# Causal attention in a post-norm decoder layer: scores computed once, by query rows in 32-row array tiles, and the softmax weights turned by DMA

## The chip, the cores and the metric

The kernel runs on one core of a Trainium2 chip. The metric is the device time of one execution in microseconds; lower is better. The five engines that matter are TensorE (PE), VectorE (DVE), ScalarE (ACT), GpSimd (POOL) and SyncE (SP), each with its own in-order instruction stream; they meet in semaphores. Moves between memories, and transposes done on the way, are DMAs.

## The reference

A decoder layer on `x` (4 x 512 x 512) in fp32: causal self-attention with 16 heads of 32, cross-attention with a 512 x 256 context, and a gated feed-forward with ternary weights, each followed by a residual and a layer norm.

```
Q = (X @ Wq.T + bq).reshape(B, S, H, d_head) * scale      # K likewise, V without scale
scores = jnp.einsum('bqhd,bkhd->bhqk', Q, K)
causal = jnp.tril(jnp.ones((S, S), bool))
scores = jnp.where(causal[None, None], scores, -jnp.inf)
attn = jax.nn.softmax(scores, axis=-1)
out = jnp.einsum('bhqk,bkhd->bqhd', attn, V).reshape(B, S, D)
x = _layernorm(x + out @ Wo.T + bo)
# cross-attention: energy = (ctx Wq)(ctx Wk)^T, softmax, x_m = x @ attention; x = _layernorm(x + x_m)
# ffn: xq = quantised rms_norm(x); p = silu(xq @ sign(W_g).T) * (xq @ sign(W_u).T); p @ sign(W_d).T
x = _layernorm(x + ffn)
```

## The kernel before

**Halves and steps.** The work is cut into eight steps `s`: batch `s // 2`, and in it the first or second 256 positions (`h = s % 2`). fp32 values are carried as a high and a low fp16 part, and a product is three matmuls (high x high, low x high, high x low); the helper at line 700 records all of those of the projections. Heads come in four groups `g` of four heads `j`; one group's queries and keys fill 128 partitions, 32 for each head. `gp` is a pair of groups.

**Causal attention before.** Queries and keys (`project`, `qk`) land in `qk`. SyncE then copies them (`stack`, line 635, tasks `sk`) into `st`, so that for each head 96 partitions hold high, low and high parts: one matmul with a depth of 96 gives the three products at once. The scores are computed twice. First by query rows (`score_max`, lines 753 and 757, tasks `mx`): only to get each query's maximum, which VectorE takes under the causal mask (`block_max`, line 1122). The maxima of two groups are turned by a small transpose (`maxima`, line 764, tasks `nm`), split in two, and copied as rows 96 and 97 of `st` by DMA (`shift_rows`, line 643, tasks `sh`), beside a constant on the key side (`shift_constants`). Then by key columns (`scores`, line 774, tasks `st`), with a depth of 128 that takes the maximum away in the product. ScalarE exponentiates. Where a piece has the diagonal, the result goes to `p32`, GpSimd masks it (`mask`, line 1274), ScalarE writes the high part into `ph` and GpSimd the low one. Where it has none, ScalarE exponentiates twice (`open_exponentials`, lines 960 and 961) and VectorE writes the low part (line 1060). As keys are on the partitions already, `ph` is the stationary operand of the product with `v` (`weigh`, line 795, tasks `pv`).

**The rest.** `op` is the output projection, `cp`, `en`, `xm` the cross-attention, `gg`, `uu` (line 851) and `dn` (line 866) the feed-forward; `to`, `tx`, `ta`, `tq` are DMA transposes of `ohl`, `rhl`, `ehl`, `xq`. All of SyncE's DMAs go through one queue.

**Order.** Each engine runs a list written out in the file (`PE_ORDER`, `ACT_ORDER`, ...), in which attention of one batch lies among the feed-forward of the batch before. Words are task and arguments; a number behind `@` is the PSUM bank, of which there are eight. A bank is reopened when the task that had it has been read (`freed_by`).

## Time and profile before

| | |
|---|---|
| median of 3 runs | 623.63 us (620.34 to 623.85) |
| the profiled execution | 617.3 us of span; 6.3 us less than the median run, which is the time around it |
| PE busy | 583.5 us, 95% |
| DVE busy | 487.6 us, 79% |
| ACT busy | 413.0 us, 67% |
| POOL busy | 395.0 us, 64% |
| DMA queue of SP | 36.4% of 16 engines' span |

The span is the profiled part of one execution. An engine's busy time is the union of its instructions. Matmuls are pipelined, so their mean duration is a latency, and what one costs in a stream is read from the length of a run of them. The granted clock of 1.00 is 2.4 GHz.

### The profile page before, as it was taken

What the parts mean: (1) busy time and instruction counts of PE and PEld (TensorE: products, weight loads), DVE (VectorE), ACT (ScalarE), POOL (GpSimd) and SP (SyncE); (2) the same over time, 40 slices, a digit from 0 to 9 for tenths busy, and PEclk for the clock granted to TensorE, in tenths of its full rate; (3) what the DMA queues carried; (4) which work ended last, traced back from release to release, by engine and by line L of the source; (5) the groups of instructions that cost most, each with busy time, mean ns of one, the idle gap of its engine ahead of it and who ended that gap; (6) DMA issues with size and microseconds to landing.
All of it is one profiled execution on the core that took longest, in us unless ns stands there. A gap on an engine that the chain in (4) does not pass through costs nothing.

```text
span 617.3 us, 13871 instructions
## 1 busy us (share of the span) xinstructions
PE 583.5 (95%) x5100; PEld 389.1 (63%) x5100; DVE 487.6 (79%) x1296; ACT 413.0 (67%) x773; POOL 395.0 (64%) x518
## 2 busy tenths in 40 slices
PE   5699789999999999989999999999999999999996
PEld 4466556547766667747666676786666667685572
DVE  3767677798998966688799886778798898787775
ACT  5849979946676776945675977655656778854151
POOL 9343966655676867665875894626876667767443
PEclk9999869999999999999999999999999999999999
DMA  8867952594024321163312520044122431032000
GB/s 302 323 206 230 253 174 53 129 256 86 10 47 105 91 70 37 49 158 91 78 39 46 146 69 19 3 103 120 36 51 53 105 87 36 10 90 56 19 35 34
DMA packets 90851, 60.29 MB, mean 98 GB/s; under 512 B 65056, under 2 KB 81952, under 8 KB 89248
## 3 DMA queue, kind: packets, MB, share of 16 engines
q1 hardware_dynamic: 90240, 58.89, 36.4%
q8 instruction: 40, 0.66, 0.5%
q10 hardware_dynamic: 544, 0.52, 0.3%
q14 instruction: 27, 0.22, 0.1%
HBM read 27.79 MB, written 4.19 MB: 52 GB/s over the span
## 4 chain that ended last, share of the span: by engine, by line
PE 66%; SPq 11%; DMA 6%; DVE 6%; ACT 6%; issue 3%; POOL 2%; ACTq 0%; POOLq 0%; DVEq 0%
PE ps_b L700 24%; PE ps_b L851 16%; PE ps_b L866 14%; SPq L635 9%; PE ps_b L795 4%; PE ps_b L774 4%; PE ps_b L757 2%; DMA st<-qk 2%; PE ps_b L753 1%; DMA oT<-ohl 1%; DMA bx<-in_b_x_dram 1%; DVE ps_b L1122 1%; ACT ps_b L961 1%; ACT p L947 1%; ACT ph L884 1%
## 5 line engine op out<-in xcount | busy, mean ns | idle before, releaser
L1122 DVE CUSTOM_DVE_ANT_0 ps_b<-ps_b,future 128x256 f32<-128x256 f32 (+3 forms) x256 | 118.7, 517 | 16.9 <-PE ps_b L757 10.4
L1317 POOL TENSOR_TENSOR ph<-p,ph 128x512 f16<-128x512 f32 x96 | 110.0, 1161 | 27.2 <-ACT ph L884 26.5
L851 PE MATMUL ps_b<-xqT,sg 128*128 128x256 f16 x1024 | 124.9, 272 | 0.1
L866 PE MATMUL ps_b<-sd,hp 128*128 128x512 fp8e4 x512 | 119.1, 379 | 0.0
L1313 POOL TENSOR_TENSOR hp<-gt,hp 128x512 f16<-128x512 f32 x64 | 74.0, 1161 | 56.6 <-ACT hp L884 56.2
L851 PEld LDWEIGHTS ps_b<-xqT,sg 128*128 128x128 fp8e4 x1024 | 98.0, 98 | 19.0 <-ACT p L947 0.6
L700 PE MATMUL ps_b<-xhl,wh 128*128 128x256 f16 x480 | 84.8, 275 | 1.4 <-DVE wl L1073 1.3
L866 PEld LDWEIGHTS ps_b<-sd,hp 128*128 128x128 f16 x512 | 48.6, 98 | 50.0 <-POOL hp L1313 1.5
L1274 POOL TENSOR_SCALAR_AFFINE_SELECT p<-p 128x256 f32<-128x256 f32 (+1 forms) x96 | 46.5, 494 | 46.2 <-ACT p L947 45.7
L700 PE MATMUL ps_b<-xhl,wl 128*128 128x256 f16 x240 | 66.0, 275 | 0.0
L947 ACT ACTIVATE p<-ps_b 128x512 f32<-128x512 f32 x96 | 54.1, 594 | 16.8 <-PE ps_b L774 16.5
L884 ACT ACTIVATE ph<-p 128x512 f16<-128x512 f32 x96 | 58.0, 634 | 9.3 <-POOL p L1274 9.0
L884 ACT ACTIVATE hp<-gt 128x512 f16<-128x512 f32 x64 | 39.9, 628 | 30.8 <-DVE gt L1239 28.1
L1060 DVE TENSOR_TENSOR ph<-ps_b,ph 128x512 f16<-128x512 f32 x64 | 43.2, 685 | 20.9 <-ACT ps_b L961 20.9
L774 PE MATMUL ps_b<-st 128*128 128x256 f16 (+1 forms) x384 | 53.9, 260 | 1.7 <-DVE tops L1122 1.2
L1032 ACT ACTIVATE gt<-gt 128x512 f32<-128x512 f32 x64 | 40.1, 626 | 19.5 <-DVE gt L1226 18.9
L700 PEld LDWEIGHTS ps_b<-xhl,wh 128*128 128x128 f16 x480 | 47.3, 99 | 9.1 <-DVE wl L1073 1.9
L1231 DVE SCALAR_TENSOR_TENSOR gt<-gt,ps_b 128x512 f32<-128x512 f32 x64 | 43.6, 682 | 11.6 <-ACT gt L1032 11.0
L1226 DVE TENSOR_TENSOR gt<-ps_b,invb 128x512 f32<-128x512 f32 x64 | 43.6, 686 | 9.6 <-POOL hp L1313 5.9
L795 PEld LDWEIGHTS ps_b<-v,ph 128*128 128x128 f16 x1376 | 46.4, 97 | 6.4 <-DVE tops L1122 1.2
L795 PE MATMUL ps_b<-v,ph 128*128 128x65 f16 (+2 forms) x1376 | 48.5, 184 | 0.5 <-DVE ph L1060 0.3
L1239 DVE SCALAR_TENSOR_TENSOR gt<-gt,ps_b 128x512 f32<-128x512 f32 x64 | 43.1, 682 | 5.4 <-PE ps_b L851 4.5
(122 smaller groups left out, 1139.6 us busy)
## 6 DMA issues: line engine op xcount, KB each, us to landing
st<-qk SPq DMA_DIRECT2D x192, 64.0 KB, 2.0
hp<-in_sgT_dram SPq DMA_DIRECT2D x6, 1024.0 KB, 6.8
gt<-in_sgT_dram SPq DMA_DIRECT2D x6, 1024.0 KB, 6.0
rows<-in_x_dram SPq DMA_DIRECT2D x8, 512.0 KB, 3.8
out_dram<-rows SPq DMA_DIRECT2D x16, 256.0 KB, 2.1
xin<-in_xT_dram SPq DMA_DIRECT2D x14, 256.0 KB, 4.5
e<-in_ctxT_dram SPq DMA_DIRECT2D x4, 512.0 KB, 4.2
hp<-in_wT_dram SPq DMA_DIRECT2D x4, 256.0 KB, 4.4
```

The costliest lines, as they stand in the source:

```text
L635: sp.dma_start(st[DH * r:DH * (r + 1), q:k + 1:k - q, j, :, :], qk[DH * j:DH * (j + 1), gp, first:first + step + 1:step, :, :])\
L700: ins = pe.matmul(ps, lhs(hl, c), rhs(hr, c), start=n == 0, stop=n == len(todo) - 1)
L774: ins = pe.matmul(ps[:, col:col + HALF - first], st[:, Q_SLOTS + 2 * gp + kt // 2, j, g % 2, kt % 2 * P:(kt % 2 + 1) * P], st[:, (2 * s + ...
L795: ins = pe.matmul(ps[:, col:col + width], ph[:, n % PH_SLOTS, half, at:at + P], v[:, kt, HG * g + j, first:first + width], start=kt == hal ...
L851: ins = pe.matmul(ps[:, a * HALF:(a + 1) * HALF], sg[:, ("gg", "uu").index(name), c, ht * P:(ht + 1) * P], xqT[:, c, :], start=c == 0, sto ...
L866: ins = pe.matmul(ps[:, :], hp[:, (UNITS * s + n) % HP_SLOTS, h, a, t * P:(t + 1) * P], sd[:, ht, :], start=ht == h == 0, stop=ht == HT - ...
L884: act.activation(out_, in_, ACT.Copy, scale=scale).then_inc(signal, 1)
L947: act.activation(p32[:, m % P32_SLOTS, :], ps[:, :], ACT.Exp, scale=EXP_SCALE).then_inc(p_exp.sem, 1)
L1122: ins = dve.tensor_tensor_reduce(scores, scores, future[:, S - width:S], 1.0, -3e38, ALU.add, ALU.max, tops[:, g // 2, j:j + 1, g % 2, qt ...
L1274: pool.affine_select(out=blocks, in_=blocks, pattern=[[0, len(cols)], [1, P]], compare_op=ALU.is_ge, fill=0.0, base=0, channel_multiplier= ...
L1313: pool.tensor_tensor(slot[:, 1, :, :], tg[:, n % 2, :, :], slot[:, 0, :, :], ALU.subtract)\
L1317: pool.tensor_tensor(out_, in_, hi, ALU.subtract).then_inc(signal, 1)
```

## The change

Scores are computed once, by query rows. There is no stacking: the three products are three matmuls with a depth of 32, each on one head's 32 partitions, and the four heads of a group follow each other, in four row tiles of the array and into four banks. Wq and bq are taken with a minus sign, so that VectorE's reduction (a minimum now) gives the exponential's bias as it is; its masked and scaled scores go back to PSUM, and ScalarE exponentiates those with the bias. Two heads make a pair (`pair`): one `p32` slot, one high part (ScalarE writes that of pair 0, VectorE that of pair 1) and one low part (GpSimd). As the queries are on the partitions now, SyncE turns both halves by one DMA transpose for each pair (`turn_weights`, tasks `tp`) into `pt`, which is what `weigh` reads. Gone are `stack`, `maxima`, `shift_rows`, `mask`, `open_exponentials`, and the second set of scores. All order lists are written anew. The buffers change with it: `p32` has 3 slots, `ph` 3, `pt` 5.

```diff
-Q_SLOTS, K_SLOTS = 3, 4
-P32_SLOTS, PH_SLOTS, HP_SLOTS = 4, 10, 6
+Q_SLOTS, K_SLOTS = 2, 3
+P32_SLOTS, PH_SLOTS, PT_SLOTS, HP_SLOTS = 3, 3, 5, 6
+FIRST_WIDTH = P + HALF
+def tiles_of(s, i):
+    return ((0, 0, P), (1, P, HALF)) if s % 2 == 0 else ((3 - i, 0, (4 - i) * P),)
+def width_of(s, i):
+    return FIRST_WIDTH if s % 2 == 0 else (4 - i) * P
...
             if name == "mx":
-                return bm_red, 0, before(MX_PIECES, s, *parts) + 1
+                return p_exp, 0, pieces_to(s, *parts) + 1
...
         def ph_free(eng, n):
 
             if n >= PH_SLOTS:
-                s0, g0, k0 = place_of(n - PH_SLOTS)
-                wait(eng, pv_done, s0, HG * g0 + LAST_HEAD[s0 % 2][k0] + 1)
+                wait(eng, turned[(n - PH_SLOTS) % PT_SLOTS], (n - PH_SLOTS) // PT_SLOTS, 16)
...
-            def stack(s, gp, j):
...
-            def shift_rows(s, gp):
...
+            def turn_weights(s, g, i, pair):
+                n, blocks = pairs_to(s, g, i, pair), 4 * width_of(s, i) // P
+                wait(sp, p_lo, 0, n + 1)
+                if n >= PT_SLOTS:
+                    s0, g0, _, pair0 = pair_at(n - PT_SLOTS)
+                    wait(sp, pv_done, s0, HG * g0 + 2 * pair0 + 2)
+                sp.dma_start_transpose(pt[:, n % PT_SLOTS, 0:blocks, :], ph[:, n % PH_SLOTS, 0:blocks * P])\
+                  .then_inc(turned[n % PT_SLOTS].sem, 16)
...
+            def scores(s, g, i):
+                h = s % 2
+                wait(pe, qk_lo, s, 2 * g + 2)
+                banks = [open_bank(("mx", s, g, HG * i + j)) for j in range(HG)]
+                for qt, col, width in tiles_of(s, i):
+                    for hq, hk in ((0, 0), (0, 1), (1, 0)):
+                        for kh in range((width + HALF - 1) // HALF):
+                            keys = min(width - kh * HALF, HALF)
+                            first = hq == hk == kh == 0 and col == 0
+                            last = hq == 1 and kh == (width - 1) // HALF and col + width == width_of(s, i)
+                            for j in range(HG):
+                                mine = slice(DH * j, DH * (j + 1))
+                                ins = pe.matmul(banks[j][:, col + kh * HALF:col + kh * HALF + keys],
+                                                qs[mine, s % Q_SLOTS, g, hq, qt % 2 * P:(qt % 2 + 1) * P],
+                                                ks[mine, (s - h + kh) % K_SLOTS, g, hk, 0:keys],
+                                                start=first, stop=last, skip_group_check=True)
+                                if last:
+                                    done(ins, ("mx", s, g, HG * i + j))
...
+                    n = pairs_to(s, g, (3 - qt) * h, j // 2)
+                    wait(pe, turned[n % PT_SLOTS], n // PT_SLOTS, 16)
                     for kt in range(qt + 1):
-                        k, at = p_block(h, j, kt, qt)
-                        n = before(ST_PIECES, s, g, k)
-                        wait(pe, *low_of(n))
                         for half, first, width in products_of:
-                            ins = pe.matmul(ps[:, col:col + width], ph[:, n % PH_SLOTS, half, at:at + P],
+                            ins = pe.matmul(ps[:, col:col + width], pt[:, n % PT_SLOTS, p_block(s, j, qt, kt, half), :],
...
             def exponentials(s, g, k):
+                i, j = divmod(k, HG)
+                n, width = pairs_to(s, g, i, j // 2), width_of(s, i)
+                act.wait_ge(*filled("mx", s, g, k))
+                ps = bank_of("mx", s, g, k)
+                wait(act, bm_red, 0, pieces_to(s, g, k) + 1)
+                wait(act, p_lo, 0, n - P32_SLOTS + 1)
+                for qt, col, keys in tiles_of(s, i):
+                    to = j % 2 * width + col
+                    ins = act.activation(p32[:, n % P32_SLOTS, to:to + keys], ps[:, col:col + keys], ACT.Exp, scale=-1.0,
+                                         bias=tops[:, s % 2, g, j, qt % 2:qt % 2 + 1])
+                ins.then_inc(p_exp.sem, 1)
...
-            def open_exponentials(s, g, k):
...
             def block_max(s, g, k):
+                i, j = divmod(k, HG)
...
+                if s >= 2:
+                    wait(dve, p_exp, 0, pieces_to(s - 2, g, HG * (1 + s % 2)))
+                for qt, col, width in tiles_of(s, i):
                     scores = ps[:, col:col + width]
-                    ins = dve.tensor_tensor_reduce(scores, scores, future[:, S - width:S], 1.0, -3e38, ALU.add, ALU.max,
-                                                   tops[:, g // 2, j:j + 1, g % 2, qt % 2])
+                    ins = dve.tensor_tensor_reduce(scores, scores, future[:, S - width:S], EXP_SCALE, 3e38, ALU.add, ALU.min,
+                                                   tops[:, s % 2, g, j, qt % 2:qt % 2 + 1])
                 ins.then_inc(bm_red.sem, 1)
...
+            def p_high(s, g, i, pair):
+                n, width = pairs_to(s, g, i, pair), 2 * width_of(s, i)
+                wait(dve, p_exp, 0, pieces_to(s, g, HG * i + 2 * pair + 2))
+                ph_free(dve, n)
+                dve.tensor_copy(ph[:, n % PH_SLOTS, 0:width], p32[:, n % P32_SLOTS, 0:width]).then_inc(p_hi[1].sem, 1)
...
-            def mask(s, g, k):
...
+            def p_low(s, g, i, pair):
+                n, width = pairs_to(s, g, i, pair), 2 * width_of(s, i)
+                wait(pool, p_hi[pair], 0, n // 2 + 1)
+                hi, lo = (ph[:, n % PH_SLOTS, half * width:(half + 1) * width] for half in range(2))
+                low(lo, p32[:, n % P32_SLOTS, 0:width], hi, p_lo.sem)
```

Two pieces of the new PE list show the two kinds of surroundings (`mx` with its four banks):

```
mx0.1.1.0@6,0,1,5 pv0.0.3.0@7 pv0.0.3.1@7 pv0.0.3.2@7 pv0.0.3.3@7 qk1.0.0@2 mx0.1.1.1@7,6,4,3 qk1.0.1@0 qk1.0.2@5
...
dn0.1.0.0@1 va1.1.1@2 mx1.1.1.0@4,3,5,6 dn0.1.0.1@1 uu0.1.4@7 uu0.1.7@3 op1.0.0@5 mx1.1.1.1@2,6,7,0 pv1.1.0.0@4
```

## Rows read from the trace of the kernel before

**Rows 1.** The page: busy time, share of the span, instructions of each engine.

```profile
PE 583.5 (95%) x5100; PEld 389.1 (63%) x5100; DVE 487.6 (79%) x1296; ACT 413.0 (67%) x773; POOL 395.0 (64%) x518
```

**Rows 2.** Windows: busy time of each engine in a stretch, TensorE clock, DMA share.

```profile
core 0: us, PE busy (x) PEld busy (x) DVE busy (x) ACT busy (x) POOL busy (x), PEclk, DMA share, GB/s
0.00:120.00 120.00, 97.84 (x899) 65.70 (x900) 81.65 (x246) 95.85 (x177) 74.56 (x83) 0.94 0.70 210
120.00:560.00 440.00, 434.37 (x3892) 292.80 (x3888) 365.69 (x976) 297.86 (x567) 294.26 (x396) 1.00 0.32 75
560.00:617.00 57.00, 51.31 (x318) 30.61 (x316) 40.26 (x75) 19.30 (x31) 26.16 (x41) 0.98 0.12 33
```

**Rows 3.** Windows again, two shorter stretches.

```profile
60.00:90.00 30.00, 24.66 (x237) 16.39 (x237) 22.20 (x73) 25.29 (x47) 23.50 (x29) 0.77 0.87 241
...
300.00:400.00 100.00, 99.26 (x942) 67.05 (x940) 86.08 (x206) 74.93 (x144) 72.08 (x95) 1.00 0.23 56
```

**Rows 4.** Timeline of PE: start us, length us, then the run of like matmuls.

```profile
341.53 0.39 PE L774 MATMUL ps_b<-st 128*128 128x128 f16 x4
...
547.57 1.79 PE L795 MATMUL ps_b<-v,ph 128*128 128x65 f16 x60
...
583.26 13.26 PE L851 MATMUL ps_b<-xqT,sg 128*128 128x256 f16 x120
...
600.69 10.62 PE L866 MATMUL ps_b<-sd,hp 128*128 128x512 fp8e4 x48
```

**Rows 5.** Groups of PE: busy us, mean ns of one.

```profile
L851 PE MATMUL ps_b<-xqT,sg 128*128 128x256 f16 x1024 | 124.9, 272 | 0.1
L851 PEld LDWEIGHTS ps_b<-xqT,sg 128*128 128x128 fp8e4 x1024 | 98.0, 98 | 19.0 <-ACT p L947 0.6
...
L764 PE MATMUL ps_b<-ident,tops 128*16 128x128 f32 x16 | 4.4, 273 | 0.2
```

**Rows 6.** Windows of the instructions on tile st alone, from 120 us on.

```profile
120.00:617.00 497.00, 75.08 (x520) 42.70 (x520) 0.00 (x0) 1.00 0.29 71
```

**Rows 7.** Groups of DVE, ACT and POOL by form: busy us, mean ns of one.

```profile
L1060 DVE TENSOR_TENSOR ph<-ps_b,ph 128x512 f16<-128x512 f32 x64 | 43.2, 685 | 20.9 <-ACT ps_b L961 20.9
L1209 DVE TENSOR_SCALAR scaled<-rows,amax 128x512 f32<-128x512 f32 x16 | 8.6, 538 | 0.6
...
L884 ACT ACTIVATE ph<-p 128x512 f16<-128x512 f32 x96 | 58.0, 634 | 9.3 <-POOL p L1274 9.0 <-PE ps_b L795 0.2
L947 ACT ACTIVATE p<-ps_b 128x512 f32<-128x512 f32 x96 | 54.1, 594 | 16.8 <-PE ps_b L774 16.5
L961 ACT ACTIVATE ps_b<-ps_b 128x512 f32<-128x512 f32 x64 | 38.7, 605 | 0.0
L884 ACT ACTIVATE invb<-ps_b 128x256 f32<-128x256 f32 x8 | 3.1, 382 | 8.0 <-PE ps_b L840 6.7 <-DVE gt L1226 1.3
...
L1317 POOL TENSOR_TENSOR ph<-p,ph 128x512 f16<-128x512 f32 x96 | 110.0, 1161 | 27.2 <-ACT ph L884 26.5
L1274 POOL TENSOR_SCALAR_AFFINE_SELECT p<-p 128x256 f32<-128x256 f32 (+1 forms) x96 | 46.5, 494 | 46.2 <-ACT p L947 45.7
```

**Rows 8.** DMA issues: count, KB each where shown, median us from issue to landing.

```profile
st<-qk SPq DMA_DIRECT2D x192, 64.0 KB, 2.0
...
oT<-ohl SPq DMA_TRANSPOSE x16, 3.3
...
xqT<-xq SPq DMA_TRANSPOSE x16, 2.4
```

**Rows 9.** SyncE's issuing instructions: min, median, max ns, first and last start.

```profile
L635 SPq DMA_DIRECT2D st<-qk x192: 585/597/1647, 26.8 to 483.1; - x192
...
L646 SPq DMA_TRANSPOSE oT<-ohl x16: 1232/1302/1977, 105.1 to 554.3; - x16
```

**Rows 10.** The chain that ended last, in order of time, 27 to 49 us: two pieces.

```profile
42.51 0.61 SPq L635
43.16 6.06 DMA st<-qk
```

More of the change, by code:

```diff
@@ new lines, in width_of, with pieces_to, pairs_to, pair_at @@
+def width_of(s, i):
+    return FIRST_WIDTH if s % 2 == 0 else (4 - i) * P
+def pieces_to(s, g, k):
+    per = (HG, 2 * HG)
+    return NG * (s // 2 * sum(per) + s % 2 * per[0]) + g * per[s % 2] + k
+def pairs_to(s, g, i, pair):
+    per = (2, 4)
+    return NG * (s // 2 * sum(per) + s % 2 * per[0]) + g * per[s % 2] + 2 * i + pair
+def pair_at(n):
+    b, n = divmod(n, NG * 6)
+    h = int(n >= NG * 2)
+    g, n = divmod(n - h * NG * 2, 2 + 2 * h)
+    return 2 * b + h, g, *divmod(n, 2)
+def p_block(s, j, qt, kt, half):
+    blocks = width_of(s, 3 - qt) // P
+    first = 0 if s % 2 or qt == 0 else 1
+    return (2 * half + j % 2) * blocks + first + kt
@@ L347, in read_order @@
             args = (2 * args[0] + args[1], *args[2:])
-        steps.append((word[:2], args, int(bank) if bank else None))
+        steps.append((word[:2], args, tuple(map(int, banks.split(","))) if banks else ()))
     return steps
@@ L354, in place_uses @@
     place, users, fills = {}, [[] for _ in range(8)], [0] * 8
-    for name, args, bank in order:
-        if bank is None:
-            continue
-        task = (name, *args[:2]) if name in ("pv", "dn") else (name, *args)
-        if task not in place:
-            fills[bank] += name not in ("pv", "dn")
-            place[task] = (bank, len(users[bank]), fills[bank])
-            users[bank].append(task)
+    for name, args, banks in order:
+        for j, bank in enumerate(banks):
+            task = (name, *args[:2]) if name in ("pv", "dn") else (name, *args)
+            if name == "mx":
+                task = (name, *args[:2], HG * args[2] + j)
+            if task not in place:
+                fills[bank] += name not in ("pv", "dn")
+                place[task] = (bank, len(users[bank]), fills[bank])
+                users[bank].append(task)
     return place, users
@@ L545, in at @@
                 return 1
-        def low_of(n):
-            where = place_of(n)
-            return p_lo if has_diagonal(where[0], where[2]) else q_lo, 0, among(*where) + 1
         def blocks_of(ps, first, blocks, width):
@@ L963, in low_products @@
+            def p_high(s, g, i, pair):
+                n, width = pairs_to(s, g, i, pair), 2 * width_of(s, i)
+                wait(act, p_exp, 0, pieces_to(s, g, HG * i + 2 * pair + 2))
+                ph_free(act, n)
+                split(ph[:, n % PH_SLOTS, 0:width], p32[:, n % P32_SLOTS, 0:width], p_hi[0].sem)
             def low_products(s, g):
@@ L1268, in _ @@
         def _(pool):
-            def mask(s, g, k):
-                m = among(s, g, k)
-                wait(pool, p_exp, 0, m + 1)
-                cols = [col for _, _, col in ST_PIECES[s % 2][k]]
-                blocks = p32[:, m % P32_SLOTS, :].rearrange("p (n q) -> p n q", n=len(cols))[:, :, 0:P]
-                pool.affine_select(out=blocks, in_=blocks, pattern=[[0, len(cols)], [1, P]], compare_op=ALU.is_ge,
-                                   fill=0.0, base=0, channel_multiplier=-1).then_inc(p_mask.sem, 1)
             def spread(s, t):
```

612 lines of the change are left out of this document (225 added, 387 removed).

## The prediction

> **What bounds the kernel now.** First the busy times [rows 1]: PE at 95% is far ahead of DVE at 79%. A mean over the span can hide stages, so next the windows [rows 2]. From 120 to 560 us PE is busy 434.4 of 440 us at the full clock: there it is the bound, with nothing to fill. In the first 120 us it idles 22.2 us, and in the last 57 us, feed-forward and last norm of the last half, 5.7 us. Two shorter windows [rows 3] say what stands behind PE: at 300 to 400 us DVE is busy 86%, ACT 75%, POOL 72%; and from 60 to 90 us, where the first attention runs with little else, PE has 82% and the clock fell to a mean of 0.77, between the levels 1.2 and 2.4 GHz, after PE had idled. So TensorE time taken away between 120 and 560 us is worth its full length as long as DVE and the chains between the engines let PE stay dense; what is taken away before 120 us is worth little.
>
> **What a matmul costs in a stream.** Durations are latencies (272 ns for 256 columns [rows 5]), so I read lengths of runs [rows 4]. 120 matmuls of 256 columns take 13.26 us; less one latency, (13.26 - 0.27) / 119 = 0.109 us each. 48 of 512 columns take 10.62 us, 0.22 each, twice that (0.218). 128 columns: 0.055, and four take 0.39 = 3 x 0.055 + 0.22, the last one's latency. 60 of 65 columns or fewer take 1.79 us: 0.027 each beside a tail of 0.2. As each of these has a weight load of its own, 0.027 us is also the least that a pair of load and matmul costs here.
>
> **Removed from PE.** For each of 64 heads and batches, row scores had one matmul of 512, two of 256 and two of 128 columns, column scores four of 256 and two of 128. 64 x 0.218 + 384 x 0.109 + 256 x 0.055 = 14.0 + 41.9 + 14.1 = 70.0 us. 16 turns of the maxima (`nm`), 0.11 each in a stream, at most their latency of 0.273 [rows 5]: 1.8. Together 71.8 us.
>
> **Added to PE.** A batch and group has 24 matmuls of 32 rows in the first half (12 of 128 columns, 12 of 256) and 48 in the second (12 of 128, 36 of 256): 1152 in all, in 288 rounds of four heads, 192 rounds of 256 and 96 of 128 columns. No matmul of the trace runs in a 32-row tile, so I bound this from both sides. If the four of a round run side by side, a round of 256 costs what one such matmul costs, 0.109 us, and it can't issue faster than 4 x 0.027 = 0.108: 0.109. A round of 128 then costs 0.108 by issue, 0.055 by columns. 192 x 0.109 + 96 x 0.108 = 31.3 us; low end 192 x 0.109 + 96 x 0.055 = 26.2. If the four run one after another, 768 x 0.109 + 384 x 0.055 = 104.8. I take 31.3: heads differ in rows of the array and in banks, so nothing that they write or hold is shared.
>
> **Going in and out of tiles.** 48 steps of scores lie among full-array matmuls, so the array changes its shape 96 times. The trace has no such change. Below, it costs nothing. Above, the full matmul before must end, 0.272 - 0.109 = 0.163 us beyond its stream price, and the next weight load (0.098 [rows 5]) is no longer hidden: 0.261. I take the first part, 96 x 0.163 = 15.6 us, since the loads fill rows that are free by then; ends 0 and 25.1. For this a rule exists: the Trainium skill, TensorEngine Tiling (Array Packing), Key Properties, says that changing the tiling mode drains TensorE. It speaks against the change as interleaved here; without it the sum would be better by those 15.6 us. A second one speaks against full overlap: the Trainium skill, TensorE: Matmul & The Clock Gate, Measured speedup vs the span model, has 3.07x for four row tiles; by that, my estimate is 104.8 / 3.07 = 34.1 us in place of 31.3. No row here shows either.
>
> So PE does 31.3 + 15.6 = 46.9 in place of 71.8: **-24.9 us**, ends -45.6 (26.2, no drain) and -15.4 (31.3 and 25.1). Of the 704 removed score matmuls 520 lie behind 120 us [rows 6], 74%: **-18.4 us** in the dense part; the other 6.5 fall where PE has idle time to spare, and I count them as nothing.
>
> **The other engines** [rows 7]. DVE: off go 64 low parts at 0.685 (43.8) and 16 maxima at about 0.27 (4.3). The 256 reductions keep their widths. On come 48 copies of 768 (32) and 1024 columns (16); the nearest row, 512 columns in 0.538, scales to 0.81 and 1.08: 43 us (if a plain copy were twice as fast, 22). DVE stays at 483 us, 82% of a shorter span. ACT: off go 96 x 0.594 + 96 x 0.634 + 64 x 1.21 + 4 = 199; on come 64 exponentials of each of 128, 256, 384 and 512 columns (from 0.594 and 0.382 by width, 0.28 + 0.38 + 0.49 + 0.59), 111, and 48 high parts at 0.85 to 1.06, 44: -44 us, off the path. POOL: off go 96 masks (96 x 0.494 = 47) and 96 x 1.161 = 111; on come 64 x 1.74 + 32 x 2.32 = 186 at most, in proportion to width: +27, 422 us, 70%. None of them overtakes PE. ACT's two added waits (`bm_red`, then `p_lo`) stand ahead of FFN work in its list, as does DVE's wait for ScalarE's exponentials of two halves before; that last one has long been met.
>
> **The queue of SyncE.** Off go 192 stack copies at 0.60 of issue (115 us) and 32 of maxima (19) [rows 9]; on come 96 transposes at 1.30 (125): even. Moved data: a transpose of 4 blocks lands after 2.4 us, one of 8 after 3.3 [rows 8], some 0.2 us for a block, so 12 blocks land after some 4.2 us and 16 after 5.1. 1280 new blocks are up to 256 us of the DMA engines, against a share of 0.32 in use in the dense part: up to 0.75, less the stacks. That hides. In the first 120 us it doesn't quite: the share is 0.70, 84 us [rows 2], for the sign matrices are loaded then; the first batch brings 320 blocks, 64 us, for stacks that took perhaps 12; that is 136 us of demand in 120. Part can slip behind 120 us; I put **+4 us**, ends 0 and +16. Against it, the first scores no longer wait for the last of the stacks in the chain: issues from 27 to 43 us and then 6.06 us of landing [rows 10]. The wait for the projections remains, so I take **-4 us**, ends 0 and -6.
>
> **Waits added.** A weight now passes reduction, exponential, high part, low part, issue and a landing of some 4 to 5 us before `pv`. SyncE's `turn_weights` waits for GpSimd's low part, and behind it in one queue stand `tq` and `to`, for which `gg` and `op` wait, and loads of `x`. A `ph` slot is held for about 1.06 + 2.32 + 1.3 + 5.1 = 9.8 us, three slots give a pair every 3.3 us; a batch has 24 pairs, 78 us in some 145, enough but not idle. Four banks at once are held through four reductions. In the dense part PE idles 1.3% now; I let that rise by a percent, **+4 us**.
>
> **The sum.** 617.3 - 18.4 + 4 - 4 + 4 = 602.9 us of span, and with 6.4 us around it (623.6 less 617.3): **609 us**, 2.3% under the median. 1% is about what a measurement of this kernel can tell from no change.
>
> **The rivals.** (1) *The shape changes cost nothing* and rounds of 128 run at column pace. Then the whole -45.6 stands, 34 of it in the dense part, and the time is about 617.3 - 34 + 4 + 6.4 = 594. For it: tiles of other rows can load while the last full matmul drains. Against: DVE, 86% at 300 to 400 us, would be the next bound.
>
> (2) *PE starves in the dense part*: the long way from scores to `pv`, with three slots and one in-order queue for all transposes, opens gaps wherever another engine runs late. It decides from the point where the idle time between 120 and 560 us grows from 5.6 by more than the 18.4 us that are saved, to above 24, or 5.5%. PE's idle share between 0 and 120 us is 18.5%, and between 60 and 90 us, where attention alone feeds it, also 18%; if the attention stretches of the later batches had 7% of idle over the 440 us, that is 31 us, 25 more than now: 617.3 - 18.4 + 25 + 6.4 = 630, slower than before. For it: five engines in a row for each pair, and the clock that fell after idle time [rows 3]. Against: some 55% of PE's work is feed-forward and projection, which the lists lay between the steps.
>
> (3) *The row tiles don't overlap*: 104.8 + 15.6 in place of 71.8 is +48.6 us, all of it on PE: 617.3 + 48.6 + 6.4 = 672. Nothing in this trace speaks against it but that the banks and rows are separate.
>
> **How the numbers follow.** Forecast (600 to 622): 0.45. Rival 1 (580 to 600): 0.15. Rival 2 (613 to 645): 0.27. Rival 3: 0.13. The range of 8 in 10 leaves rival 3 out, and tips of the others: 583 to 643. Faster by over 1% (under 617.4): 0.38 + 0.15 + 0.02 = 0.55. Within 1%: 0.07 + 0.07 = 0.14. Slower (over 629.9): 0.18 + 0.13 = 0.31. The forecast's and rival 1's own range is 583 to 620.
>
> **What would show it.** The form 32*128 in the groups of PE: in its timeline, four such matmuls of 256 columns per 0.11 us, or per 0.44 if rival 3 holds; a gap of some 0.16 us at each end of a step. Windows 120 to 560 us: PE busy near 97% is the forecast; under 94% is rival 2, and then the waits of PE name `pt` or the banks of the scores. The DMA share there near 0.6. DVE near 483, POOL near 420, ACT near 370 us. It would be wrong most simply if a short matmul in a tile can't issue at 0.027 us: each 0.01 us more for one is 11.5 us.

## The result: 0.8% slower

| | before | after |
|---|---|---|
| median of 5 runs each | 621.45 us (620.34 to 623.85) | 626.21 us (624.83 to 627.64) |
| profiled execution, span | 617.3 us | 624.2 us |

The ratio is 1.0079, with an interval of 1.0051 to 1.0107: slower, by less than the 1% called "within" in the prediction, which had forecast 609 us, against a median before of 623.6 (three runs then, five now). The first line of the page answers to [rows 1], the windows to [rows 2] and [rows 3] (share of DMA engines in the last column but one, after the granted clock):

```profile
PE 552.5 (89%) x5532; PEld 352.1 (56%) x5532; DVE 494.7 (79%) x1264; ACT 396.3 (63%) x741; POOL 408.1 (65%) x421
...
q1 hardware_dynamic: 240768, 88.11, 70.0%
```

```profile
core 0: us, PE busy (x) PEld busy (x) DVE busy (x) ACT busy (x) POOL busy (x), PEclk, DMA share, GB/s
0.00:120.00 120.00, 88.13 (x895) 56.45 (x896) 75.77 (x216) 89.75 (x159) 56.66 (x53) 0.86 1.01 256
120.00:560.00 440.00, 406.36 (x4287) 261.69 (x4286) 374.07 (x968) 284.25 (x547) 320.10 (x324) 0.99 0.71 128
560.00:624.00 64.00, 58.03 (x354) 33.92 (x352) 44.90 (x82) 22.29 (x35) 31.35 (x45) 1.00 0.13 38
...
60.00:120.00 60.00, 40.65 (x447) 25.63 (x448) 32.66 (x88) 38.84 (x57) 31.15 (x22) 0.74 1.10 235
120.00:140.00 20.00, 11.49 (x183) 8.59 (x182) 15.41 (x54) 14.94 (x25) 15.08 (x18) 0.74 0.88 155
240.00:320.00 80.00, 70.41 (x852) 45.19 (x850) 70.59 (x210) 51.37 (x109) 61.72 (x67) 1.00 0.86 152
```

PE's busy time shrank as meant, 583.5 to 552.5 us, 31.0 less, and the span still grew by 6.9: the idle time of PE grew by 37.9. Of that, 28.0 lie between 120 and 560 us (440 - 406.4 = 33.6 in place of 5.6) and 9.7 in the first 120 us (31.9 in place of 22.2), where the clock's mean is 0.86 and the DMA engines have no time left (share 1.01). The worst stretch behind that is the next one, 120 to 140 us: 8.5 of 20 us idle, at a clock of 0.74. Later the idle time is spread; from 240 to 320 us it is 9.6 us, and no other engine is full there (DVE 88%, POOL 77%).

The new matmuls, first in PE's timeline (start, length, count of a run), then by form, as in [rows 4] and [rows 5]:

```profile
301.68 0.50 PE L704 MATMUL ps_b<-v,pt 128*128 128x65 f16 x12 [0.50 <-DVE ks L1004]
302.11 0.83 PE L682 MATMUL ps_b<-ks,qs 32*128 32x256 f16 x24
302.87 0.54 PE L704 MATMUL ps_b<-v,pt 128*128 128x65 f16 x14
...
447.02 0.27 PE L626 MATMUL ps_b<-xhl,wl 128*128 128x256 f16 x1
447.13 0.27 PE L626 MATMUL ps_b<-xhl,wh 128*128 128x256 f16 x1
447.33 0.67 PE L682 MATMUL ps_b<-ks,qs 32*128 32x128 f16 x24
447.94 0.28 PE L626 MATMUL ps_b<-xhl,wh 128*128 128x256 f16 x1
```

```profile
L682 PE MATMUL ps_b<-ks,qs 32*128 32x256 f16 x768 | 34.3, 289 | 17.6 <-DVE o L1043 8.1 <-ACT p L853 8.0 <-DVE gt L1126 0.8
L682 PE MATMUL ps_b<-ks,qs 32*128 32x128 f16 x384 | 15.4, 224 | 2.2 <-DVE rows L1073 1.0 <-DVE rows L1142 0.8 <-ACT p L853 0.3
```

24 tile matmuls of 256 columns, six rounds of four heads, stand 0.76 us before the next full-array matmul starts; at 0.109 a round they need 0.65. So the four run side by side, and going out of the tiles leaves 0.11 us. Going in costs about as much and lies before the first tile matmul: at 447 us the full-array matmuls of 256 columns start 0.11 us apart, and the first tile matmul starts 0.20 us after the last of them, 0.09 later than in a stream. So a change of shape costs some 0.1 us here, not 0.163. The second step (its row names the first form only) has three rounds of 128 columns and three of 256 in 0.61 us; less 3 x 0.109 and the 0.11 for going out, a round of 128 takes some 0.06 us, the pace of its columns (0.055) and not the 0.108 taken for issue.

What waits, and for what: SyncE's queue, then DVE, then PE (us in total, times, longest).

```profile
SPq L568 <- POOL ph L1203: 146.7, 64, 12.8
...
DVE gt L1121 <- POOL hp L1199: 19.0, 27, 1.7
...
PE ps_b L682 <- ACT p L853: 8.3, 4, 5.6
PE ps_b L682 <- DVE o L1043: 8.1, 2, 6.1
PE ps_b L704 <- DMA pt<-ph: 6.8, 7, 3.2
```

The turns themselves, as in [rows 9] (issue in ns: min, median, max), and the groups of GpSimd, VectorE and ScalarE that stand before them, as in [rows 7]:

```profile
L568 SPq DMA_TRANSPOSE pt<-ph x96: 1274/1776/8447, 38.2 to 542.2; - x96
...
DMA to landing us min/median/max: 3.6/4.3/10.4
```

```profile
L1203 POOL TENSOR_TENSOR ph<-p,ph 128x768 f16<-128x768 f32 x64 | 105.6, 1653 | 40.6 <-ACT ph L793 22.6 <-DVE ph L1030 17.9
...
L1203 POOL TENSOR_TENSOR ph<-p,ph 128x1024 f16<-128x1024 f32 x32 | 68.7, 2148 | 28.9 <-ACT ph L793 21.4 <-DVE ph L1030 7.5
...
L1030 DVE CAST ph<-p 128x768 f16<-128x768 f32 x32 | 28.0, 876 | 8.0 <-ACT p L853 5.3 <-DMA pt<-ph 2.6
L1030 DVE CAST ph<-p 128x1024 f16<-128x1024 f32 x16 | 20.2, 1264 | 5.5 <-ACT p L853 5.4
...
L853 ACT ACTIVATE p<-ps_b,tops 128x512 f32<-128x512 f32 x64 | 41.8, 686 | 22.8 <-DVE tops L1022 9.8 <-issue 5.0 <-POOL ph L1203 4.6
```

SyncE's one queue stands 146.7 us before the turns (L568), waiting for GpSimd's low parts, and behind each such wait are `tq`, `to`, `tx` and the loads of `x`. A queue that stands has lost nothing by that alone: in the kernel before it waited for GpSimd as well, 54.2 us for the low parts of `rhl` alone. The three waits of PE are 23 us of the 71.7 that it idles; its idle time is spread over many names, so the waits alone don't say which link to shorten. Experiments have to.

### The profile page after: what moved, and what is told of

Same layout as the page of the kernel before. It is cut to its first block and busy times, and to the rows that moved or that the text cites. A ratio compares the mean times of both kernels' runs of the same rounds, so it can differ in the third digit from the quotient of the medians.

```text
span 624.2 us, 14611 instructions
## 1 busy us (share of the span) xinstructions
PE 552.5 (89%) x5532; PEld 352.1 (56%) x5532; DVE 494.7 (79%) x1264; ACT 396.3 (63%) x741; POOL 408.1 (65%) x421
## 5 line engine op out<-in xcount | busy, mean ns | idle before, releaser
L1203 POOL TENSOR_TENSOR ph<-p,ph 128x768 f16<-128x768 f32 (+1 forms) x96 | 174.1, 1818 | 69.5 <-ACT ph L793 43.9
L853 ACT ACTIVATE p<-ps_b,tops 128x128 f32<-128x128 f32 (+3 forms) x256 | 119.9, 535 | 51.4 <-DVE tops L1022 27.5
L1022 DVE CUSTOM_DVE_ANT_0 ps_b<-ps_b,future 128x128 f32<-128x128 f32 (+3 forms) x256 | 117.9, 518 | 17.5 <-PE ps_b L682 17.3
L760 PE MATMUL ps_b<-xqT,sg 128*128 128x256 f16 x1024 | 119.7, 273 | 4.5 <-DVE o L1043 1.0
L1199 POOL TENSOR_TENSOR hp<-gt,hp 128x512 f16<-128x512 f32 x64 | 76.1, 1196 | 47.6 <-ACT hp L793 47.6
L704 PE MATMUL ps_b<-v,pt 128*128 128x65 f16 (+2 forms) x1376 | 48.4, 186 | 16.1 <-DMA pt<-ph 6.8
L704 PEld LDWEIGHTS ps_b<-v,pt 128*128 128x128 f16 x1376 | 44.9, 98 | 30.1 <-ACT p L853 9.6
L793 ACT ACTIVATE hp<-gt 128x512 f16<-128x512 f32 x64 | 39.9, 628 | 33.6 <-DVE gt L1134 32.4
L1030 DVE CAST ph<-p 128x768 f16<-128x768 f32 (+1 forms) x48 | 48.2, 1005 | 13.6 <-ACT p L853 10.7
L682 PE MATMUL ps_b<-ks,qs 32*128 32x256 f16 (+1 forms) x1152 | 38.2, 267 | 19.8 <-ACT p L853 8.3
L626 PE MATMUL ps_b<-aT,x1T 128*128 128x512 f16 x192 | 45.5, 392 | 1.3 <-ACT p L853 0.7
L793 ACT ACTIVATE ph<-p 128x768 f16<-128x768 f32 (+1 forms) x48 | 44.2, 921 | 0.2
```

What stands on the lines that cost most here:

```text
L626: ins = pe.matmul(ps, lhs(hl, c), rhs(hr, c), start=n == 0, stop=n == len(todo) - 1)
L704: ins = pe.matmul(ps[:, col:col + width], pt[:, n % PT_SLOTS, p_block(s, j, qt, kt, half), :], v[:, kt, HG * g + j, first:first + width], ...
L760: ins = pe.matmul(ps[:, a * HALF:(a + 1) * HALF], sg[:, ("gg", "uu").index(name), c, ht * P:(ht + 1) * P], xqT[:, c, :], start=c == 0, sto ...
L793: act.activation(out_, in_, ACT.Copy, scale=scale).then_inc(signal, 1)
L853: ins = act.activation(p32[:, n % P32_SLOTS, to:to + keys], ps[:, col:col + keys], ACT.Exp, scale=-1.0, bias=tops[:, s % 2, g, j, qt % 2:q ...
L1022: ins = dve.tensor_tensor_reduce(scores, scores, future[:, S - width:S], EXP_SCALE, 3e38, ALU.add, ALU.min, tops[:, s % 2, g, j, qt % 2:qt ...
```

## Experiments

Ratios are to the kernel before, in runs on the same chip; times are medians. The changed kernel stands at 626.2 (1.0079, interval 1.0051 to 1.0107), the one before at 621.5. The experiments ran on several chips, on which the kernel before had medians of 620.3 to 621.6 us; where two kernels below differ by less than about 3 us and their intervals overlap, the difference isn't shown.

### Which part of the changed kernel costs: one at a time

**quarter_turns** turns 4 blocks in place of 12 or 16, so that `pv` reads the wrong blocks.

```diff
-sp.dma_start_transpose(pt[:, n % PT_SLOTS, 0:blocks, :], ph[:, n % PH_SLOTS, 0:blocks * P])
+sp.dma_start_transpose(pt[:, n % PT_SLOTS, 0:4, :], ph[:, n % PH_SLOTS, 0:4 * P])
```

> Leaves out: each weight transpose moves only its first 4 blocks of 12 or 16, and the weighted sums read those 4 again and again. All waits, issues and matmuls stay. Theory A (the volume of the transposes is what starves PE: DMA share above 1.0 up to 120 us, 0.71 behind it): the DMA share falls to about 0.4, the waits of the weighted sums for pt go, and the time falls from 626 to 600 us or less. Theory B (the chain of reduction, exponential, high and low part on DVE, ACT and POOL starves it): within 5 us of 626, only the first 140 us gain a little. Theory C (PE itself): no change.

623.35 us, 1.0025 (1.0002 to 1.0048). The DMA share from 120 to 560 us fell to 0.37 and SyncE's issue by a third, which answers to the row of L568 above:

```profile
L568 SPq DMA_TRANSPOSE pt<-ph x96: 1188/1190/2905, 38.0 to 538.8; - x96
```

Two thirds and more of the moved data and some 80 us of issue (203.5 to 121.8 in sum) are worth 2.9 us. Neither is the main cost. The number of turns stayed the same, so what it costs to have them at all isn't tested by this.

**low_narrow** computes 128 columns of GpSimd's low parts in place of 768 or 1024 (the rest stay 0).

```diff
-low(lo, p32[:, n % P32_SLOTS, 0:width], hi, p_lo.sem)
+low(lo, p32[:, n % P32_SLOTS, 0:P], hi, p_lo.sem)
```

> Leaves out: GpSimd's low parts of the weights are written for 128 columns only, in place of 768 or 1024 (about 174 us of POOL become 96 x 0.5 = 48). Theory A (DMA volume): within 5 us of 626, for the same bytes are turned. Theory B (chain and slots through the engines): each pair lands 1.3 to 1.8 us earlier and slots come free earlier, 605 to 615 us. Theory C (PE): no change.

604.89 us, 0.9711 (0.9672 to 0.9750): 21.3 us gained. GpSimd's low parts, by form, fell from 174.3 us in two rows to one of 41.5:

```profile
L1204 POOL TENSOR_TENSOR ph<-p,ph 128x128 f16<-128x128 f32 x96 | 41.5, 434 | 127.2 <-ACT ph L793 83.9 <-DVE ph L1031 43.2
```

The window of 120 to 560 us then reads:

```profile
120.00:560.00 440.00, 423.62 (x4366) 272.65 (x4367) 366.96 (x982) 289.67 (x558) 220.45 (x327) 0.99 0.70 129
```

and SyncE's wait for it to:

```profile
SPq L568 <- POOL ph L1204: 108.1, 50, 11.1
```

PE idles 16.4 us in the dense part where it was 33.6. Work of an engine that was busy 65% of the span is worth most of all that was tried here. But the edit did more than it says. VectorE's busy time fell too, from 494.7 to 476.5 us, though its work was not cut. Its copies of the high parts (L1030 above, 876 and 1264 ns) got shorter:

```profile
L1031 DVE CAST ph<-p 128x768 f16<-128x768 f32 x32 | 20.7, 646 | 6.9 <-ACT p L853 5.4 <-DMA pt<-ph 1.3
L1031 DVE CAST ph<-p 128x1024 f16<-128x1024 f32 x16 | 11.9, 745 | 5.7 <-ACT p L853 5.4 <-DMA pt<-ph 0.2
```

The timeline of the changed kernel shows it one by one: a copy beside a subtraction of GpSimd takes 2.61 us, the same copy with GpSimd idle 0.68.

```profile
255.41 2.13 POOL L1203 TENSOR_TENSOR ph<-p,ph 128x1024 f16<-128x1024 f32 x1
255.48 2.61 DVE L1030 CAST ph<-p 128x1024 f16<-128x1024 f32 x1
...
310.62 0.68 DVE L1030 CAST ph<-p 128x1024 f16<-128x1024 f32 x1
311.38 2.13 POOL L1203 TENSOR_TENSOR ph<-p,ph 128x1024 f16<-128x1024 f32 x1 [1.79 <-DVE ph L1030]
```

Of the 48 copies, the 14 that met no work of GpSimd took 0.55 to 0.56 us (768 columns) and 0.68 to 0.69 (1024); the other 34 took 1.04 and 1.40 in the mean. So GpSimd's load acts in two ways, by its own lateness and by stretching VectorE's copies.

**copy_narrow** does the same to VectorE's high parts (`p_high`), **one_product** leaves out two of the three score products, 768 of the 1152 tile matmuls.

```diff
-dve.tensor_copy(ph[:, n % PH_SLOTS, 0:width], p32[:, n % P32_SLOTS, 0:width]).then_inc(p_hi[1].sem, 1)
+dve.tensor_copy(ph[:, n % PH_SLOTS, 0:P], p32[:, n % P32_SLOTS, 0:P]).then_inc(p_hi[1].sem, 1)
```

```diff
-for hq, hk in ((0, 0), (0, 1), (1, 0)):
+for hq, hk in ((0, 0),):
```

> Leaves out: VectorE's copies into the high part of every second pair are 128 columns wide (48 us of DVE become about 12). DVE is busy 85% behind 120 us and over 90% in attention stretches. If DVE is what now sets the pace, 36 us less of it bring the time to 600 to 610 us. Theory A (DMA volume): 621 to 628 us. Theory C (PE): no change.

> Leaves out: of the three products of a score (high x high, high x low, low x high) only the first; 384 tile matmuls in place of 1152, some 20 us less of PE. If PE still sets the pace 606 us; theories A and B: PE has idle time now, so 622 to 627 us.

copy_narrow: 618.75 us, 0.9948 (0.9924 to 0.9973), 7.5 us gained, with 15.8 us less of busy VectorE (478.9 for 494.7). one_product: 623.74 us, 1.0035 (1.0008 to 1.0063), with 16.0 us less of busy PE (536.5 for 552.5) 2.5 us gained. By what was gained the order is GpSimd, VectorE, and then DMA and TensorE, which these runs can't tell apart: the reverse of what a sum by PE time assumes. By gain for each us taken off, VectorE comes first (7.5 for 15.8), GpSimd and TensorE are level (21.3 for 133.5, 2.5 for 16.0, the latter not clear of noise).

**low_and_turns** has the edits of low_narrow and quarter_turns.

> low_narrow and quarter_turns together: what they leave out is as told there. With POOL out of the way the volume of the transposes may be next. If so 590 to 597 us; if the transposes are hidden as in quarter_turns alone, 602 to 605 us.

601.51 us, 0.9693 (0.9662 to 0.9723): 3.4 us more than low_narrow by the medians, 1.1 by the ratios, as the two ran on different chips; quarter_turns had 2.9 alone. So the transposes' data stay cheap with GpSimd out of the way too.

### Is it the change's, and is it load or lateness?

**before_low_narrow** narrows GpSimd's low parts (L1317) in the kernel before. **low_early** narrows them in the changed kernel, signals, and then gives GpSimd the rest of the load in an unused tile, so that the turn starts early but GpSimd has as much to do.

```diff
-low(lo, p32[:, n % P32_SLOTS, 0:width], hi, p_lo.sem)
+low(lo, p32[:, n % P32_SLOTS, 0:P], hi, p_lo.sem)
+k = min(width // P - 1, 6)
+wait(pool, spared, 0, n)
+pool.tensor_tensor(spare[:, 0:k, :], ident[:].unsqueeze(1).to_broadcast([P, k, P]), ones[:].unsqueeze(1).to_broadcast([P, k, P]), ALU.subtract).then_inc(spared.sem, 1)
```

> The kernel before, with GpSimd's low parts 128 columns wide in place of 512 (left out: the rest of them; 110 us of POOL become about 35). If POOL is a bound only of the changed kernel: 619 to 622 us, no change. If the kernel before has the same slack to give: 610 us or less, and the 21 us of low_narrow say nothing on the change.

> Leaves out what low_narrow does (low parts of 128 columns), but GpSimd then does as many columns again as were left out, into a spare tile for which nobody waits; the signal that the low part is there comes before. POOL carries its load of the changed kernel (a little less for the wide pairs), while each pair is turned 1.2 to 1.8 us earlier. If the load of POOL's in-order queue is the cause: 618 to 626 us, as without the edit. If the length of the way of each pair and the slots held on it are the cause: about 605 us, as low_narrow.

before_low_narrow: 620.92 us, 0.9995 (0.9972 to 1.0018), with GpSimd at 327.2 us for 395.0. GpSimd's load costs the old kernel nothing. Two things differ there, and no run tells them apart: only `weigh` waits for the weights' low parts, and no queue of DMAs; and VectorE has no copies of high parts that GpSimd could stretch. low_early: 618.36 us, 0.9958 (0.9939 to 0.9978), with GpSimd at 415.6 us and SyncE's wait for it down from 146.7 us to:

```profile
SPq L570 <- POOL ph L1206: 119.3, 57, 10.7
```

So of the 21.3 us some 7.8 (626.2 to 618.4) come from the pair's own way getting shorter, with GpSimd carrying 7.5 us more than in the changed kernel. Some 13.5 (618.4 to 604.9) go with GpSimd's load. A part of these is VectorE's: its busy time is 494.5 us in low_early and 476.5 in low_narrow, 18.0 less, and copy_narrow gained 7.5 us for 15.8. The rest is GpSimd's list being late with all that lies behind: the next pairs' low parts, `hidden_low` (`hp` L1199, for which VectorE's `gate` waits), and those of `ohl` and `rhl`, which SyncE also waits for. How they divide, stays open; `gate`'s 19.0 us fell only to 18.1 in low_narrow, so it is hardly that one.

### Other engines for the same work, and more room

**shared_low** gives pair 1 another way: ScalarE the high part, VectorE the low part. **act_high** gives ScalarE all high parts and leaves the low ones. **slots_ph** moves one slot from `pt` to `ph`. **after_less_act** narrows ScalarE's high parts (pair 0) to 128 columns.

```diff
-ex0.0.1.1 ex0.0.1.2 ex0.0.1.3 hi0.0.1.0.0 qk0.1.2
+qk0.1.1 ez0.2 ex0.0.1.1 ex0.0.1.2 ex0.0.1.3 hi0.0.1.0.0 hi0.0.1.0.1 qk0.1.2
```

```diff
-P32_SLOTS, PH_SLOTS, PT_SLOTS, HP_SLOTS = 3, 3, 5, 6
+P32_SLOTS, PH_SLOTS, PT_SLOTS, HP_SLOTS = 3, 4, 4, 6
```

```diff
-split(ph[:, n % PH_SLOTS, 0:width], p32[:, n % P32_SLOTS, 0:width], p_hi[0].sem)
+split(ph[:, n % PH_SLOTS, 0:P], p32[:, n % P32_SLOTS, 0:P], p_hi[0].sem)
```

The first is ScalarE's list, the same in shared_low and act_high but for a few places (all 48 such tasks come in, and the matching ones leave VectorE's list or become low parts there).

> Computes everything. For every second pair ScalarE writes the high part and VectorE the low one, where VectorE wrote the high part and GpSimd the low one: some 87 us less on POOL, 44 us more on ACT, DVE about even. The lists of POOL and SP are else as in the changed kernel; in those of ACT and DVE the two tasks were put where they first can run. If GpSimd's 174 us of low parts are what takes the gain away (126 us less of them gave 21 us), half of it comes back: 606 to 616 us, faster than both kernels. If the time came only from the low part being short for each pair, whoever writes it, 610 to 618. If DVE or ACT are as close to the bound as POOL, 620 us or more.

> Computes everything. The high part of every second pair is written by ScalarE too, in place of VectorE: 48 us less on DVE, 44 us more on ACT, POOL as in the changed kernel. ScalarE's list has the task where it first can run. In shared_low the same move, with the low part taken from POOL to DVE, cost 26 us. If ScalarE's in-order list is what that kernel lost on: 640 us or more here. If the loss there was VectorE's, with its low part behind ScalarE's high: here 615 to 626 us.

> Computes everything. Four slots of ph in place of three, paid for in SBUF by four of pt in place of five. If the three slots between high part and transpose hold pairs up: 615 to 622 us. If not, 624 to 628 us, or more where four slots of turned weights are too few.

> The changed kernel, with ScalarE's high parts of the first pairs 128 columns wide (left out: the rest; 48 x 0.92 become 48 x 0.32, 29 us less of ACT). act_high put 44 us on ACT and took 48 off DVE for a loss of 6 us. If ScalarE counts in the way of each pair: 612 to 618 us. If ACT's load is free, 624 to 627 us, and the loss of act_high came from where its tasks lie.

shared_low: 652.59 us, 1.0513 (1.0475 to 1.0551). GpSimd has 78 us less (330.3 for 408.1), and it is 26 us slower. act_high: 632.16 us, 1.0163 (1.0116 to 1.0209); VectorE has 36 us less, ScalarE 38 more, and it is 6 us slower. slots_ph: 636.59 us, 1.0239 (1.0196 to 1.0283), 10 us slower. after_less_act: 626.14 us, 1.0099 (1.0069 to 1.0128), nothing, with 26.5 us less on ScalarE (369.8).

Less load on ScalarE gains nothing and more of it costs. Whether that is the load or the place of the added tasks in a list that runs strictly in order (a high part that waits for its pair holds the next exponentials), these runs can't say. slots_ph's waits of SyncE show what it traded away:

```profile
SPq L568 <- POOL ph L1203: 120.9, 56, 12.8
SPq L460 <- PE ps_b L704: 55.7, 15, 21.9
```

SyncE waits 26 us less for GpSimd, but with four slots of `pt` it now waits 55.7 us, in L568's task, for `weigh` (L704) to free one. Same queue, another wait.

### Was TensorE the bound before?

**before_less_pe** and **after_less_pe** leave out one of three products (that of the activations' low half) in the output projection `op` and in the product of `x1T` and `aT` of the cross-attention (`xm`): 128 matmuls of 512 columns, 128 x 0.218 = 27.9 us at the price of a stream. **before_less_dve** narrows VectorE's low part (L1060), **before_less_act** ScalarE's high part of the weights (L884) to 128 columns, **before_less_pe_dve** is the first and the third together.

```diff
-                todo = [(c, h) for c in range(terms) for h in ((0, 0), (1, 0), (0, 1))]
+                todo = [(c, h) for c in range(terms) for h in pairs]
...
+                              lambda h, c: w_half[h][:, 3, c, :], pairs=((0, 0), (0, 1))), ("op", s, t))
```

```diff
-low(ph[:, n % PH_SLOTS, 1, :], bank_of("st", s, g, k)[:, :], ph[:, n % PH_SLOTS, 0, :], q_lo.sem)
+low(ph[:, n % PH_SLOTS, 1, 0:P], bank_of("st", s, g, k)[:, 0:P], ph[:, n % PH_SLOTS, 0, 0:P], q_lo.sem)
```

> The kernel before without the product low x high in the output projection and in the cross-attention product (left out: 128 matmuls of 512 columns, 128 x 0.218 = 27.9 us of PE; nothing else changes). If PE is the bound of the kernel before, 593 to 600 us, nearly 1 us for each us. If other engines and chains stand close behind, so that no saving on PE can show in it: 610 us or more, and the score tiles would have met the same wall whatever they replaced.

> The changed kernel with the same 27.9 us of PE left out (the same product in the same two places). If it is starved and no longer bound by PE: 615 to 624 us, less than half of what the kernel before gains. If PE still sets its pace where these matmuls lie: 600 us or less.

> The kernel before, with VectorE's low parts of the open pieces 128 columns wide in place of 512 (left out: the rest; 64 x 0.685 become 64 x 0.3, 25 us less of DVE). PE's and POOL's loads proved free there. If VectorE is what sets the pace of the kernel before: 598 to 608 us. If it is a loop in which no single engine is the bound: 612 to 620 us.

> The kernel before, with ScalarE's high parts of the masked pieces 128 columns wide in place of 512 (left out: the rest; 96 x 0.634 become 96 x 0.32, 30 us less of ACT). If ScalarE sets the pace: 595 to 605 us; if the loop is shared: 612 to 620 us; if its share is nothing: 621.

> The kernel before with both before_less_pe (27.9 us less of PE) and before_less_dve (25 us less of DVE). If PE is a bound that stands level with DVE's, so that neither alone gives anything, both together give 15 to 25 us: 597 to 606 us. If PE counts for nothing, the time is that of before_less_dve.

| kernel | less work by the page | us | ratio (interval) |
|---|---|---|---|
| before_less_pe | PE 564.6 for 583.5 | 621.46 | 0.9992 (0.9961 to 1.0023) |
| before_less_dve | DVE 468.5 for 487.6 | 621.00 | 1.0000 (0.9975 to 1.0024) |
| before_less_act | ACT 385.8 for 413.0 | 623.40 | 1.0044 (1.0018 to 1.0071) |
| before_less_pe_dve | PE 565.0, DVE 469.4 | 618.39 | 0.9968 (0.9929 to 1.0006) |
| after_less_pe | PE 532.0 for 552.5 | 624.18 | 1.0058 (1.0033 to 1.0083) |

The first row decides most. In the kernel before, 98.7% busy between 120 and 560 us, 28 us of TensorE's work are worth nothing. In the changed kernel they are worth 2.0 us, less than these runs can tell from nothing. Both edits take matmuls out of the output projection and the cross-attention, while the change took them out of the scores. That the scores' matmuls too were worth nothing is argued from this; no run shows it by itself. The same window in before_less_pe:

```profile
120.00:560.00 440.00, 414.56 (x3714) 278.54 (x3712) 363.11 (x970) 294.17 (x563) 288.80 (x390) 0.99 0.32 74
```

and one of PE's waits:

```profile
PE ps_b L753 <- DMA st<-qk: 4.8, 4, 2.2
```

The time became idle time in the same window, 25.4 us for 5.6, and its scores now wait for the stacks: L753's wait for `st<-qk` was 0.6 us before, and L757's rose from 5.3 to 8.3 us. PE was full, but it did not set the pace alone; something else, as long, ran beside it. Nor was it the low parts of VectorE or the high parts of ScalarE alone: narrowing either gave nothing.

### What set the pace then

The page of the kernel before names a candidate that the prediction read only for its first 49 us: the chain that ended last, by engine.

```profile
PE 66%; SPq 11%; DMA 6%; DVE 6%; ACT 6%; issue 3%; POOL 2%; ACTq 0%; POOLq 0%; DVEq 0%
```

In before_less_pe, where the time stayed, half of PE's share has gone to all the others:

```profile
PE 33%; DVE 16%; SPq 15%; ACT 12%; POOL 10%; DMA 7%; issue 6%; POOLq 0%; DVEq 0%; ACTq 0%
```

**before_one_stack** makes one of the three stack copies (the others' rows of `st` stay at constants, so the low halves' products of the self-attention scores are left out; PE does the same work), **before_one_stack_less_pe** adds the edit of before_less_pe.

```diff
-                for r, (first, step) in enumerate(((0, 2), (1, 1), (0, 3))):
+                for r, (first, step) in enumerate(((0, 2),)):
```

> The kernel before with one stack copy for each head and pair of groups in place of three (left out: the low parts of queries and keys in the scores, which are zero or a constant there; 128 of 192 issues of 0.6 us and of 64 KB each on SyncE's queue, 77 us of issue; the matmuls keep their shapes). If SyncE's queue alone sets the pace of the kernel before: 600 us or less. If it stands level with PE: 612 to 621 us. If it is hidden altogether: 621 us.

> The same with 27.9 us less of PE, as in before_less_pe. If PE and SyncE's queue stand level, each hiding the other, both together give what neither does: 595 to 605 us. If 615 us or more, the wall behind PE is neither, and it stays open which loop it is.

before_one_stack: 610.27 us, 0.9825 (0.9777 to 0.9873). before_one_stack_less_pe: 604.49 us, 0.9732 (0.9692 to 0.9772). In before_one_stack, SyncE's remaining copies, the chain that ended last by engine, and the first two windows:

```profile
L636 SPq DMA_DIRECT2D st<-qk x64: 585/597/1832, 27.5 to 469.4; - x64
```

```profile
PE 72%; ACT 8%; POOL 6%; DVE 6%; DMA 3%; issue 3%; SPq 1%; POOLq 0%; ACTq 0%; DVEq 0%
```

```profile
0.00:120.00 120.00, 102.31 (x964) 68.22 (x965) 84.56 (x266) 99.68 (x181) 75.59 (x84) 0.96 0.63 193
120.00:560.00 440.00, 436.95 (x3874) 295.21 (x3873) 370.19 (x970) 296.58 (x569) 297.08 (x400) 1.00 0.26 62
```

128 issues fewer (64 in place of 192, 40.5 us in place of 120.5) give 10.6 us, with TensorE, VectorE, ScalarE and GpSimd doing all they did: the first 120 us hold 102.3 us of PE in place of 97.8 [rows 2]. That stretch, which the prediction had called worth little, is where PE's idle time fell most, by 4.5 us (22.2 to 17.7); in the dense part it fell from 5.6 to 3.1. And only now is TensorE's work worth something: the same 27.9 us give 5.8, a fifth of their length. So SyncE's copies were one partner of PE, and something else is close behind: which, stays open. The copies' data and their landing went too. The share of the DMA engines fell only from 0.32 to 0.26 in the dense part and from 0.70 to 0.63 in the first 120 us; that the issue and not the data or the landing paid is argued from that, and not shown.

## Why the prediction was wrong

**The step that failed** is "TensorE time taken away between 120 and 560 us is worth its full length", with the condition that the chains let PE stay dense, and the +4 us for that condition. PE's busy time fell by more than forecast, 31.0 us for 24.9, and it brought no gain. That is not the added waits alone: before_less_pe took 27.9 us off PE without any of them, and gained 0. A busy share of 98.7% had been read as proof of a bound. It proves only that PE wasn't waiting; after a little was taken away, it waited. The idle time in the dense part rose by 28.0 us, not by 4.

**Rival 2** named what happened: decides above 18.4 us of added idle time in the dense part, gives 630 for 25 us. Measured: 28.0 us, 626.2. But its mechanism was only partly right. It said long way, three slots and one queue, where "another engine runs late", and had no engine for it. The engine is GpSimd (21.3 us by low_narrow), which the prediction had dismissed at 70% busy with "None of them overtakes PE". The same GpSimd edit gives 0 in the kernel before, so it is the change that makes it matter: it put SyncE's one queue behind GpSimd for each pair, and it gave VectorE copies that GpSimd's work stretches. Which of the two costs more isn't shown. The prediction did list the waits of `turn_weights`, and what stands behind; it gave them 4 us, the percent for all waits. The stretched copies it didn't have at all. And "even" for SyncE's queue compared issue with issue, 134 us for 125, where the stacks' removal is by itself a gain in the old kernel (10.6 us for two thirds of them) and the turns bring a new in-order wait.

Two sizes side by side, not an experiment: with two thirds of the stacks and 28 us of TensorE gone the old kernel takes 604.5 us; with GpSimd's low parts and the turns cut down the new one takes 601.5. Both leave work out, GpSimd's above all in the second, so they show what the waits of the new kernel can cost, up to 24.7 us from 601.5 to 626.2, and not what the change would gain without them.

**Term by term.**
- Overlap: rounds of four side by side, as taken; rival 3 is out. The Trainium skill, TensorE: Matmul & The Clock Gate, Measured speedup vs the span model, has 3.07x; here six rounds took 0.65 us where 24 such matmuls in a row would take 24 x 0.109 = 2.6, so 4x, and 3.1x with the 0.2 us of both shape changes counted: with these the trace agrees. The rounds of 128 columns ran at some 0.06 us, so the prediction's low end of 26.2 us for the tiles was nearer than the 31.3 that it took.
- Shape changes: some 0.1 us each, not 0.163; for 96 of them 10 us, and 15.6 was some 6 too much. That matmuls pause at a change of shape agrees with the drain of the Trainium skill, TensorEngine Tiling (Array Packing), Key Properties. By these two sizes, an estimate, PE's work is 26.2 + 10 = 36 us in place of 71.8: about 36 less, where the busy time shows 31.0. Rival 1's sizes were about half right, and its time of 594 us didn't follow, as nothing on PE was worth its length.
- Start: forecast +4 and -4. The demand was there (share 1.01 for "136 of 120"), PE idles 9.7 us more in the first 120 us and 8.5 in the 20 behind them, and the clock's mean is 0.86 in place of 0.94. The shorter way to the first scores didn't cover it.
- Issue of a turn of 12 or 16 blocks: median 1.78 us, up to 8.4, 203.5 us in sum; forecast 1.30 and 125. It had been taken from 8 blocks [rows 9]. By quarter_turns this was worth at most 2.9 us. Landing: 4.3 us, in the forecast's 4.2 to 5.1.
- DVE: 494.7 for 483 (and 483 of 602.9 us is 80%, not the 82% written; the time around the span is 6.3 us, not 6.4; neither matters). Its copies took 48.2 us for 43. Left alone by GpSimd they would take 32 x 0.557 + 16 x 0.687 = 28.8, an estimate from the 14 that were: nearly the half that the prediction left open, so the size was right by luck. ACT: 396.3 for 370; its exponentials with a bias from `tops` took 384, 491, 580 and 686 ns for the four widths, each some 0.1 us more than the 280, 380, 490 and 590 of the forecast, 26 us over 256 of them. POOL: 408.1 for 422. DMA share: 0.71 for 0.6.
- What it said would show rival 2, PE's share under 94% from 120 to 560 us, with waits on `pt` or the scores' banks, is what the trace shows: 92.4%, L704 on `pt<-ph`, L682 on ScalarE's reads of its banks.

**What stays open**: which loop paces the changed kernel once GpSimd is relieved (601.5 us, PE still idle 14 us in the dense part); how GpSimd's 13.5 us divide among those who wait for its list and VectorE's stretched copies; load against placement on ScalarE. No version that computes all of the reference and beats the kernel before was found. The one direction that the runs recommend, fewer or cheaper DMA issues in the old kernel, was tried only with work left out.

## What to carry to other kernels

Before pricing a change at the length of the work that it takes off the busiest engine, take that much off in some other way and time it: a full engine can have a partner just as long, here in part a queue of small DMAs that no busy row counts. Read the whole chain that ended last by engine and add up its shares of queues. When a change lets an in-order queue wait for an engine, count that engine as on the path, however idle its row looks. And when an edit that leaves work out of one engine gives more than expected, compare the means of the other engines' rows: here GpSimd's work had been making VectorE's copies longer.
